# Input chunks in four slots, x1 in the memory of x2's high part, and the row below added by a transfer

## The reference, cut to what matters

```python
# 1: a five-point stencil with reflected edges, and a reaction term
x = x + zX * (left - 2 x + right) + zY * (above - 2 x + below) + zR * x * (1 - x)      # gives x1
# 2: attention pooling under one of three masks; scores = tanh(x W1 + b1) . v
x = x + softmax(mask(scores)) @ x / count                                             # gives x2
# 3: a linear layer chosen by subject
x = x + x @ weight[subject].T + bias[subject]                                         # gives x3
# 4: a bottleneck adapter chosen by profile, and a normalisation
y = x + relu(x @ down_w + down_b) @ up_w + up_b
x = x + layernorm(y) * g + b
```

## Time and profile before

| | |
|---|---|
| time, median of 3 runs | 703.36 us (699.14, 703.36, 703.60) |
| profiled execution | 703.28 us, its span 701.6 us |
| mean granted TensorE clock | 0.949 |
| busy PE / DVE / POOL / ACT | 572.5 / 537.7 / 358.2 / 324.1 us |
| moved from and to HBM | 99.4 MB, mean 142 GB/s |

### The profile page before, as it was taken

The page is one execution under the profiler, slowest core; times in us unless marked ns, Lnnn a source line. Parts: engine busy times, 40 slices in busy tenths (PEclk is TensorE's granted clock), DMA queues, the critical chain, the costliest instruction groups (busy, mean ns, idle before and its releaser), DMA issues.

```text
span 701.6 us, 10274 instructions
## 1 busy us (share of the span) xinstructions
PE 572.5 (82%) x2928; PEld 457.0 (65%) x2928; DVE 537.7 (77%) x1149; ACT 324.1 (46%) x545; POOL 358.2 (51%) x263
## 2 busy tenths in 40 slices
PE   0247768979799788879889798898899798999992
PEld 0125646768668676668758676577768686688771
DVE  4565768699968998599968998498977899567422
ACT  1253445344745456235555266244564357543431
POOL 7242662348617565257636566075653678127232
PEclk9998889999999999899999999998999899999996
DMA  5471047325693187514693277622785166334364
GB/s 196 156 242 68 0 167 225 120 60 118 230 284 63 39 247 193 184 45 90 221 275 109 39 203 198 214 60 47 238 226 178 30 151 222 77 76 92 75 128 83
DMA packets 62838, 99.40 MB, mean 142 GB/s; under 512 B 11040, under 2 KB 15648, under 8 KB 62800
## 3 DMA queue, kind: packets, MB, share of 16 engines
q1 hardware_dynamic: 44240, 65.42, 28.4%
q0 software_dynamic: 9344, 16.79, 17.2%
q10 hardware_dynamic: 9216, 16.78, 6.3%
HBM read 65.42 MB, written 33.55 MB: 141 GB/s over the span
## 4 chain that ended last, share of the span: by engine, by line
PE 30%; DVE 28%; issue 17%; POOL 16%; ACT 3%; DMA 1%; SPq 1%; POOLq 0%; DVEq 0%; ACTq 0%
PE y L540 9%; POOL x2l L473 7%; PE front_ps L638 5%; PE front_ps L563 5%; POOL xu L430 5%; DVE mask L1031 3%; DVE x2f L1185 3%; PE front_ps L586 3%; POOL xd L438 2%; DVE xd L1052 2%; DVE xu L1044 2%; DVE mask L1035 2%; DVE pn L1139 2%; PE front_ps L571 2%; DVE x L1059 2%
## 5 line engine op out<-in xcount | busy, mean ns | idle before, releaser
L473 POOL TENSOR_TENSOR x2l<-x2f,x2h 128x1024 fp32r<-128x1024 f32 x32 | 89.8, 2813 | 55.5 <-DVE x2f L1185 44.1
L455 POOL TENSOR_TENSOR norm<-norm 128x1 f32<-128x1 f32 x64 | 44.4, 702 | 143.1 <-DVE norm L1209 142.8
L540 PE MATMUL y<-wth,x2h 128*128 128x512 f32 x256 | 103.8, 406 | 11.0 <-DVE wtl L1151 11.0
L430 POOL TENSOR_TENSOR xu<-xu,xd 128x1024 f32<-128x1024 f32 x32 | 79.5, 2485 | 62.7 <-DMA xd<-in_x 61.6
L540 PE MATMUL y<-wtl,x2h 128*128 128x512 f32 x256 | 103.1, 403 | 0.0
L540 PE MATMUL y<-wth,x2l 128*128 128x512 f32 x256 | 102.6, 401 | 0.0
L638 PE MATMUL front_ps<-th_pt,x 128*128 128x129 f32 x512 | 76.7, 308 | 28.7 <-DVE x2f L1185 28.5
L638 PEld LDWEIGHTS front_ps<-th_pt,x 128*128 128x128 f32 x512 | 74.0, 221 | 33.6 <-DVE x2f L1185 30.8
L438 POOL TENSOR_TENSOR xd<-xn 128x1024 f32<-128x1024 f32 x32 | 66.6, 2080 | 34.0 <-ACT xn L758 30.5
L552 PE MATMUL front_ps<-ident,x 128*128 128x128 f32 x256 | 35.5, 290 | 50.3 <-DVE x L1059 50.3
L778 ACT ACTIVATE xd<-xn,cur 128x1024 f32<-128x1024 f32 x32 | 39.8, 1243 | 77.6 <-DVE xu L1044 77.6
(11 more groups left out here) (120 smaller groups left out, 1185.8 us busy)
## 6 DMA issues: line engine op xcount, KB each, us to landing
xn<-in_x SPq DMA_DIRECT2D x32, 512.0 KB
out<-x ACTq DMA_DIRECT2D x64, 256.0 KB, 2.0
out<-o_sb POOLq DMA_DIRECT2D x64, 256.0 KB, 4.4
...
```

Source lines behind the costliest of these rows:

```text
L430: pool.tensor_tensor(xu[:, sl, :, :], xu[:, sl, :, :], xd[:, sl, :, :], ALU.add).then_inc(pool_b, 1)
L473: pool.tensor_tensor(x2l[q][:, k, :], x2f[:, k % 2, :], x2h[q][:, k, :].bitcast(F32), ALU.subtract).then_inc(x2l_ready, 1)
L540: ins = mm(dst, lhs, rhs, start=first and q == 0, stop=last and q == len(parts) - 1, skip_group_check=True)
```

## The change

The chunks of x have four slots (`xn` and `xu` by chunk, `xd` still two and now only a work buffer). SP loads two copies of a chunk, not three, and as soon as the same chunk of the batch before has been diffused. The rows below are no longer loaded and added by POOL: POOL issues an adding transfer from HBM into `xu` (`add_below`), one transfer for chunks 0 to 2 and four for chunk 3. x1 has two buffers, one for each batch in turn, in the memory of `x2h`, with its columns in the order that `x2h` has them, and is overwritten by `x2h` block by block. The mask is made by a step of its own, `take_mask`, after the last chunk. On POOL, ACT and DVE the steps are in another order. PE's order is unchanged. On ACT `round_up` now follows `keep_x1t(3)`.

```diff
--- before.py
+++ after.py
@@ -100,10 +100,9 @@
         tok_f = sb("tok_f", [P, B])
         table = sb("table", [P, TABLE, B])
 
-        xn = sb("xn", [P, 2, 2, D + 2])
-        xu = sb("xu", [P, 2, 2, D])
+        xn = sb("xn", [P, NC, 2, D + 2])
+        xu = sb("xu", [P, NC, 2, D])
         xd = sb("xd", [P, 2, 2, D])
-        x1 = sb("x1", [P, NJ, D])
         cur = sb("cur", [P, TABLE])
         mask = sb("mask", [P, MASK])
         pn = sb("pn", [P, S])
@@ -116,11 +115,13 @@
         prod = sb("prod", [P, 2, NJ, NJ])
         x2f = sb("x2f", [P, 2, S])
 
-        x1t, x2h, x2l = [], [], []
+        x1, x1t, x2h, x2l = [], [], [], []
         for q in range(2):
             with nc.sbuf_tensor(f"x1t{q}", [P, KD, S], F32) as a:
                 x1t.append(a)
             x2l.append(sb(f"x2l{q}", [P, KD, S], F32R))
+            with nc.sbuf_tensor(f"x1{q}", [P, KD, NJ, P], F32) as a:
+                x1.append(a)
             x2h.append(sb(f"x2h{q}", [P, KD, S], F32R))
 
         wn = sb("wn", [P, KD, D])
...
@@ -250,7 +250,8 @@
         dve_back = sem("dve_back")
         dve_setup = sem("dve_setup")
         pool_own = sem("pool_own")
-        x_loaded = [sem("x_loaded0"), sem("x_loaded1")]
+        x_loaded = [sem(f"x_loaded{c}") for c in range(NC)]
+        below_added = [sem(f"below_added{c}") for c in range(NC)]
         base_stored = [sem(f"base_stored{i}") for i in range(XB)]
         stored = [sem(f"stored{i}") for i in range(OB)]
 
@@ -258,11 +259,8 @@
         CONST_DMAS, CONST_MADE = 7, 3
 
 
-        X_DMAS = [6] + [3] * (NC - 2) + [6]
-
-        def x_count(n, c):
-
-            return n * 16 * sum(X_DMAS[c % 2::2]) + 16 * sum(X_DMAS[c % 2:c + 1:2])
+        X_DMAS = [5] + [2] * (NC - 1)
+        BELOW_DMAS = [1] * (NC - 1) + [4]
 
         def before(t, ring):
 
@@ -308,9 +306,9 @@
 
             def load_x(n, c):
 
-                sl, r0, size = c % 2, c * 2 * P, 2 * P
-
-                wait_past(sp, l0_done, NC * n + c - 1)
+                r0, size = c * 2 * P, 2 * P
+
+                wait_past(sp, l0_done, NC * (n - 1) + c + 1)
 
                 def get(dst, lo, hi):
                     src = x[bass.ds(n, 1), lo:hi, :]
@@ -318,24 +316,16 @@
                         src = src.rearrange("b (j p) d -> p (b j) d", p=P)
                     else:
                         src = src.rearrange("b p d -> p (b d)")
-                    sp.dma_start(dst, src).then_inc(x_loaded[sl], 16)
-
-                get(xn[:, sl, :, 1:D + 1], r0, r0 + size)
+                    sp.dma_start(dst, src).then_inc(x_loaded[c], 16)
+
                 if c == 0:
-                    get(xu[1:113, sl, 0, :], 0, 112)
-                    get(xu[113:P, sl, 0, :], 112, P - 1)
-                    get(xu[0:1, sl, 0, :], 1, 2)
-                    get(xu[:, sl, 1, :], P - 1, 2 * P - 1)
-                    get(xd[:, sl, :, :], r0 + 1, r0 + 1 + size)
-                elif c == NC - 1:
-                    get(xu[:, sl, :, :], r0 - 1, r0 - 1 + size)
-                    get(xd[:, sl, 0, :], r0 + 1, r0 + 1 + P)
-                    get(xd[0:112, sl, 1, :], r0 + P + 1, r0 + P + 113)
-                    get(xd[112:P - 1, sl, 1, :], r0 + P + 113, S)
-                    get(xd[P - 1:P, sl, 1, :], S - 2, S - 1)
+                    get(xu[1:113, c, 0, :], 0, 112)
+                    get(xu[113:P, c, 0, :], 112, P - 1)
+                    get(xu[0:1, c, 0, :], 1, 2)
+                    get(xu[:, c, 1, :], P - 1, 2 * P - 1)
                 else:
-                    get(xu[:, sl, :, :], r0 - 1, r0 - 1 + size)
-                    get(xd[:, sl, :, :], r0 + 1, r0 + 1 + size)
+                    get(xu[:, c, :, :], r0 - 1, r0 - 1 + size)
+                get(xn[:, c, :, 1:D + 1], r0, r0 + size)
 
             def token(tok, n, count):
                 return sp.value_load(tok.rearrange("(o b) -> o b", o=1)[:, bass.ds(n, 1)],
@@ -423,19 +413,32 @@
                 link(pool.memset(ones[:, :], 1.0))
                 pool.memset(minus_half[:, :], -0.5).then_inc(const_made, 1)
 
-            def above_and_below(m, c):
-
-                sl = c % 2
-                pool.wait_ge(x_loaded[sl], x_count(m, c))
-                pool.tensor_tensor(xu[:, sl, :, :], xu[:, sl, :, :], xd[:, sl, :, :],
-                                   ALU.add).then_inc(pool_b, 1)
+            def add_below(m, c):
+
+                r0, size = c * 2 * P, 2 * P
+                pool.wait_ge(x_loaded[c], 16 * X_DMAS[c] * m + 16 * X_DMAS[c])
+
+                def add(dst, lo, hi):
+                    src = x[bass.ds(m, 1), lo:hi, :]
+                    if hi - lo == size:
+                        src = src.rearrange("b (j p) d -> p (b j) d", p=P)
+                    else:
+                        src = src.rearrange("b p d -> p (b d)")
+                    pool.dma_start(dst, src, accum_op=ALU.add).then_inc(below_added[c], 16)
+
+                if c == NC - 1:
+                    add(xu[:, c, 0, :], r0 + 1, r0 + 1 + P)
+                    add(xu[0:112, c, 1, :], r0 + P + 1, r0 + P + 113)
+                    add(xu[112:P - 1, c, 1, :], r0 + P + 113, S)
+                    add(xu[P - 1:P, c, 1, :], S - 2, S - 1)
+                else:
+                    add(xu[:, c, :, :], r0 + 1, r0 + 1 + size)
 
             def left_and_right(m, c):
 
-                sl = c % 2
                 pool.wait_ge(halo, NC * m + c + 1)
-                pool.wait_ge(pool_b, NC * m + c + 1)
-                pool.tensor_tensor(xd[:, sl, :, :], xn[:, sl, :, 0:D], xn[:, sl, :, 2:D + 2],
+                wait_past(pool, l0_done, NC * m + c - 1)
+                pool.tensor_tensor(xd[:, c % 2, :, :], xn[:, c, :, 0:D], xn[:, c, :, 2:D + 2],
                                    ALU.add).then_inc(pool_a, 1)
 
             def bias_rest(n, q):
...
@@ -474,49 +477,50 @@
                                    ALU.subtract).then_inc(x2l_ready, 1)
 
             def program(b, n, m, q):
+                if m is not None:
+                    add_below(m, 0)
+                    add_below(m, 1)
                 if b is not None:
                     root(b, 0)
                     root(b, 1)
                     finish(b, 0)
+                    finish(b, 1)
+                    root(b, 2)
+                if m is not None:
+                    left_and_right(m, 0)
                 if n is not None:
...
@@ -635,7 +639,7 @@
                         pe.wait_ge(alb_ready, n + 1)
                     for j in range(j0, j1):
                         o = (j - j0) * (P + 1)
-                        ins = mm(front_ps[:, GROUP_BANK[k % 2][g], o:o + P + 1], x1[:, j, blk(k)],
+                        ins = mm(front_ps[:, GROUP_BANK[k % 2][g], o:o + P + 1], x1[q][:, k, j, :],
                                  pt[:, j, :], start=True, stop=True)
                 if g == NG - 1:
                     ins.then_inc(p_mm, 1)
...
@@ -759,30 +763,27 @@
 
             def reflect(m, c):
 
-                sl = c % 2
-                act.wait_ge(x_loaded[sl], x_count(m, c))
-                copy(xn[:, sl, :, 0:D + 2:D + 1], xn[:, sl, :, 2:D:D - 3]).then_inc(halo, 1)
+                act.wait_ge(x_loaded[c], 16 * X_DMAS[c] * m + 16 * X_DMAS[c])
+                copy(xn[:, c, :, 0:D + 2:D + 1], xn[:, c, :, 2:D:D - 3]).then_inc(halo, 1)
 
             def scale_rows(m, c):
 
-                sl = c % 2
                 act.wait_ge(cur_ready, m + 1)
-                act.wait_ge(pool_b, NC * m + c + 1)
-                act.activation(xu[:, sl, :, :], xu[:, sl, :, :], ACT.Identity,
+                act.wait_ge(below_added[c], 16 * BELOW_DMAS[c] * m + 16 * BELOW_DMAS[c])
+                act.activation(xu[:, c, :, :], xu[:, c, :, :], ACT.Identity,
                                scale=cur[:, Z_Y:Z_Y + 1]).then_inc(scaled_rows, 1)
 
             def centre(m, c):
 
-                sl = c % 2
                 act.wait_ge(around, NC * m + c + 1)
-                act.activation(xd[:, sl, :, :], xn[:, sl, :, 1:D + 1], ACT.Identity,
+                act.activation(xd[:, c % 2, :, :], xn[:, c, :, 1:D + 1], ACT.Identity,
                                bias=cur[:, CENTRE:CENTRE + 1], scale=cur[:, MINUS_R:MINUS_R + 1]
                                ).then_inc(c_done, 1)
 
             def keep_x1t(n, q, c):
                 act.wait_ge(xt_ps, NC * n + c + 1)
 
-                wait_past(act, y_ps, NJ * (n - 1))
+                wait_past(act, y_ps, NJ * (n - 2) + 2 * c + 2)
                 pair = (pair_b, pair_a)[c % 2]
                 copy(x1t[q][:, :, c * 2 * P:(c + 1) * 2 * P],
                      pair[:, :].rearrange("p (k q) -> p k q", k=KD)).then_inc(x1t_ready, 1)
...
@@ -953,16 +947,14 @@
                     centre(m, 3)
                 if n is not None:
                     keep_x3(n, 0)
+                    store_base(n, 0)
                     keep_x3(n, 1)
-                    store_base(n, 0)
                     store_base(n, 1)
                 if m is not None:
+                    keep_x1t(m, 1 - q, 2)
```

(26 more changed lines are left out.)

136 lines of the change are left out of this document (63 added, 73 removed).

## The result

The changed kernel takes **717.94 us** (median of 4 runs, 716.0 to 730.8; the profiled one 716.34, span 714.7). The kernel before took 703.48 beside it. The ratio is **1.0216 [1.0179, 1.0253]**: slower, by 1.8 to 2.5%. The run of 730.8 is a slow one and stands outside that ratio. The forecast was 694 and 660 to 713. The direction was wrong, and the time lies outside the range.

What follows compares the result with a forecast made beforehand. DVE was taken to set the time from the mask to the weight's rest, though busy only 77%. From 703.3 us, -7.6 for the first call and -0.2 in each of 7 rounds gave 694, range 660 to 713.

Steps and rivals of the forecast that it cites:

- x2f was to start 6.3 us earlier: Pooling: with the mask moved to the round's end, the first x2f starts at 386.3 instead of 392.64.
- POOL's queue was to give back part of it: Ahead of the first x2l, POOL's finish and issues (4.1 us) leave 3.0 of the 6.3 us won.
- `linear(n, 0)` was to start 2.5 us later: Fourth pooling block to the weight's rest: added work and turns make PE start linear(n, 0) 2.5 us later.
- The mask at the round's end: The mask falls where DVE waits for PE, from 436 on, and costs nothing.
- The turns of DVE and POOL: Beside the third and fourth x2l, DVE's and POOL's instructions on x exclude one another, adding 2 x 1.89 us.
- the cover of the loads: Loads of chunks 0 and 1 behind the weights land by 437, before POOL's root at 439.44; fits by 2 us.
- 2 us a round (708): Rival: loads of x come late, delaying ACT's scaling and the tanh; 2 us a round, 708; chance 0.05.
- first call: Start of the kernel: earlier loads let the compute start 9.8 us earlier, of which 7.6 us are taken.
- behind `linear(n, 0)`: PE's waits for x1 (1.8), x1t (0.65) and half of 0.52 go: -2.7 us a round.
- Half speed moves: Rival: PE idles some 5 us ahead of linear(n, 0), half speed follows, costing 1.7 us; 702; chance 0.15.
- PE as the bound (662): Rival: POOL's queue keeps up, DVE keeps the mask's 6 us, PE's waits go; 662; chance 0.27.
- POOL's queue and turns: Rival: dear issues, full DVE waits for POOL and half speed, 3.1 us a round; 717, part 712; chance 0.15.

Runs made afterwards that it cites:

- e4: The kernel before with one part of the change alone: the mask made after the last chunk of x, not ahead of the pooling; 662.6 us.
- e1: The changed kernel with POOL's root of block 0 ahead of the additions of chunks 0 and 1; 703.1 us.
- e9: e5 with POOL's left_and_right(0) and (1) ahead of the additions of chunks 2 and 3 in the first call, and root(b, 4) ahead of the second x2l; 668.5 us.
- e7: e3 without the adding transfers, the rows below left out of the result; 666.1 us.
- e2: The changed kernel with POOL's issues of chunks 2 and 3 behind the first finish, and the finish of block 2 behind the first x2l; 704.6 us.
- e3: The changed kernel with the edits of both e1 and e2; 689.3 us.
- e5: e3 with POOL's left_and_right(m, 1) right behind left_and_right(m, 0); 683.7 us.

## Why the prediction was wrong

**Right in mechanism, and near in size.** x2f was to start 6.3 us earlier; it starts 6.1 earlier, and e4 shows that the mask's place is worth 6.4 us a round where nothing takes it back. POOL's queue was to give back part of it, 4.1 us for five issues with bounds of 3.7 to 4.6; they take 5.03, above the bound (1.2 for 256 rows, as taken, and 3.8 for chunk 3's four, in place of 2.8), and of the 6.1 us 1.5 are left where 3.0 were to be. `linear(n, 0)` was to start 2.5 us later within the round; in the round shown it is 2.0. The mask at the round's end was to cost nothing, and does not: DVE stands 2.02 us for PE behind it. The turns of DVE and POOL are there (2.84 for L1038 at 29.70 beside POOL's L441, 1.28 alone). The reading that DVE has no idle time from the mask to the weight's rest was a little off: it stands 1.26 us at 398.64 and 0.30 at 414.97.

**The step that failed** is the cover of the loads: "Their loads come behind the weights: 3.9 MB from 419 on ... It fits by 2 us". The second chunk was to be there at 437, 56.5 us behind the round's `alpha` transposes. It is there 60.7 to 65.1 us behind them in rounds 2 to 6. I let everything run from 419 on at 328 GB/s and did not ask what the queue waits for. These are the last rows of SP ahead of x in the round shown:

```profile
437.25 0.37 SPq L358 DMA_DIRECT2D wu<-in_L_cond_up_w  x1
440.48 0.36 SPq L362 DMA_DIRECT2D g_row<-in_L_cond_ln_g  x1
441.10 1.82 SPq L319 DMA_DIRECT2D xu<-in_x  x4
```

The marks of this round lie 11.8 us later than before, so 441.1 stands for 429.3. By the sum the weights' 1.8 MB would have been through at 424.5 (an estimate: 1.8 of the 3.9 MB at 328 GB/s from 419). The queue starts the weights 1.8 us later than 419, takes 5.1 us to issue them, and `g_row` then waits 2.9 us for the subtraction of the batch's last row block. The change itself had put that subtraction behind 2.4 us of DVE work on chunk 2; what it would give to put it back was not tested. From x's first issue to the second chunk's landing it is 11.9 us in this round, near the 12.1 of the sum, and 15.8 in the second. The fit had 2 us to spare, and behind the loads stands the root. The rival was named, with 2 us a round (708) and a chance of 0.05. It is the one that came true: e1 takes it away and gains 14.8 us (13.4 between the marks), 7.9 of them in the second round, 3.9 in the fourth and 3.0 in the first, part of that the half speed behind PE's wait. The prediction's own test, "x landed long before", shows it false.

**Mis-sized, first call.** -7.6 was -3.2. Chunk 3's load landed at 24.2 and not 20, `left_and_right(1)` stood behind its addition, and DVE's chunk 1 began at 29.7 and not 25. How much of the loss is due to that order is open: e9 has another order, and its first transposes come at 66.7, as here at 66.6. Without the additions, in e7, they come at 63.8.

**Mis-sized, behind `linear(n, 0)`: the half speed.** -2.7 a round was put there. In most rounds it was won and lost again. From the start of `linear(n, 0)` to the next `alpha` transposes, in rounds without the jump, read from PE's timelines:

| kernel and round | products of 0.63 us behind the start | stretch, us |
|---|---|---|
| before, rounds 2 and 4 | none | 36.5, 36.3 |
| e2, e3 and e5, round 7 | none | 34.2, 34.2, 34.2 |
| e1, rounds 4 and 7 | 7, 7 | 35.4, 35.5 |
| e1, rounds 2 and 6 | 11, 11 | 36.6, 36.7 |

In the changed order, at full speed, the stretch is 2.1 to 2.3 us shorter: the forecast of -2.7 was near. Products of 0.63 us follow one another at 0.43 us and not at 0.23, so seven of them cost 1.4 us and eleven 2.2 (an estimate from these rows), about what the stretches differ by. The changed kernel has 6 to 11 of them in each of rounds 2 to 7, 57 in all, and e1 has 49; the kernel before has 7 and 6 in its last two such rounds, where its stretch is no longer for them. This is the rival "Half speed moves", behind the very wait that it named, though PE stands there for 2.6 us and not for 5. The sum had put this term at nothing.

**The account.** At the last `alpha` transposes the forecast was -9.0 and the profiles give +15.3 (636.4 against 621.1). The 24.3 between them: first call 4.4, root behind the late loads 13.4, and 6.5 that e1 still lies above the forecast. These 6.5 are a net: up to the starts of `linear(n, 0)` its seven rounds are 9.1 us shorter than forecast, 5.2 of it in the first, which has no b, and behind them 15.6 longer. That the two go against each other is luck. Of the 15.6, the half speed makes 9.8 (49 products at 0.20); 3.9 more stand in the two rounds with the jump, which the prediction did not know as rounds of their own. The half speed was read from the traces; no run takes it away alone.

**The rivals.** PE as the bound (662) did not come. The number 662.6 of e4 is chance: e4 is the kernel before with another place of the mask, without the four slots and the loads ahead. What e4 does show is the part of that rival on the mask: with nothing of the change on POOL, DVE keeps its 6 us. I had seen that the mask was worth 6.3 us a round and that the rest of the change would spend it; I did not conclude that the mask alone was the better change. The rival "POOL's queue and turns" names a true cost, 3.1 us a round by e3, but the forecast has most of it already; the time of 717 that it gave came from another cause. The sign of five issues and a finish ahead of `x2l`, with DVE waiting, came true, and so did a `wtl` that starts 38 us after the first pooling block (434.45).

**The Trainium skill's rule** on descriptors ("SBUF — State Buffer", "SBUF: two separate sides") was to add some tenths of a us where POOL otherwise waits. The issue that runs beside the mask's first instruction, at 448.56, takes 1.23 us, and the one at 452.97, with no such instruction beside it, 1.21. Chunk 3's four issues take 3.49 us at 24.19, where DVE stands idle for all but the first 0.9 us, and about 3.8 of the 5.03 at 403.73, where DVE is busy. So the rule explains nothing of the miss.
